# q and k computed as two extra columns of the value projection, with row scales transposed later

## The reference

```python
h = jnp.maximum(_layernorm(x, axis=-1), 0.0)          # over the nodes
q = jnp.einsum('c,bcn->bn', wq, h)
k = jnp.einsum('c,bcn->bn', wk, h)
scores = q[:, None, :] + k[:, :, None]
scores = jnp.where(scores > 0, scores, 0.01 * scores)
att = jax.nn.softmax(scores, axis=-1)
agg = jnp.einsum('bcn,bmn->bcm', h, att)
out = jnp.einsum('oc,bcm->bom', wm, agg) + bm[None, :, None]
x = x + jax.nn.relu(out)
```

## Time and profile before

| | |
|---|---|
| median of 3 runs | 2089.28 us (2089.21 to 2089.91) |
| profiled execution | 2090.47 us, its span 2088.7 |
| TensorE busy | 2051.5 us (98%) |
| VectorE busy | 1674.8 us (80%) |
| ScalarE busy | 1221.5 us (58%) |
| GpSimd busy | 379.6 us (18%) |

### The profile page before, as it was taken

How to read it: one execution, slowest core, us unless ns; L and a number is a source line. 1 busy time by engine, 2 the same in 40 slices (tenths; PEclk the granted TensorE clock), 3 DMA queues, 4 the chain that set the end, 5 groups by cost and what they waited for, 6 DMA issues and landing times.

```text
span 2088.7 us, 33534 instructions
## 1 busy us (share of the span) xinstructions
PE 2051.5 (98%) x10448; PEld 950.3 (45%) x10448; DVE 1674.8 (80%) x3661; ACT 1221.5 (58%) x1871; POOL 379.6 (18%) x273
## 2 busy tenths in 40 slices
PE   5899999999999999999999999999999999999999
PEld 2344444444444444444444444444444444444444
DVE  7978878778887788887788877888877888778853
ACT  5556656556655566565566555665655665556634
POOL 1012211112111122111121111221111211112212
PEclk9999999999999999999999999999999999999999
DMA  5244433344324444333433234442334432343332
GB/s 195 64 155 142 148 99 123 138 160 141 133 84 136 151 141 146 104 118 137 161 141 133 84 136 151 141 146 105 117 137 161 141 131 86 136 152 141 106 101 76
DMA packets 126395, 271.46 MB, mean 130 GB/s; under 512 B 22624, under 2 KB 23136, under 8 KB 122208
## 3 DMA queue, kind: packets, MB, share of 16 engines
q1 hardware_dynamic: 123904, 269.01, 37.1%
q10 hardware_dynamic: 2400, 1.58, 0.3%
HBM read 202.91 MB, written 67.63 MB: 130 GB/s over the span
## 4 chain that ended last, share of the span: by engine, by line
PE 95%; DVE 3%; DMA 1%; POOL 0%; issue 0%; ACT 0%; POOLq 0%; SPq 0%; DVEq 0%
PE mix L385 21%; PE mix L387 21%; PE mix L386 21%; PE mix L362 10%; PE mix L363 10%; PE mix L364 10%; PE small L325 2%; DVE den_out L728 1%; PE small L334 1%; DMA xs<-in_x_dram 0%; DVE p_ring L749 0%; DVE p_lo L756 0%; DVE v_lo L761 0%; POOL wm_nat L893 0%; DMA den_row<-den_rows 0%
## 5 line engine op out<-in xcount | busy, mean ns | idle before, releaser
L385 PE MATMUL mix<-p_hi,v_hi 128*128 128x512 f16 x2048 | 776.3, 379 | 5.9 <-DVE p_lo L756 5.4
L386 PE MATMUL mix<-p_lo,v_hi 128*128 128x512 f16 x2048 | 776.2, 379 | 0.0
L387 PE MATMUL mix<-p_hi,v_lo 128*128 128x512 f16 x2048 | 776.2, 379 | 0.0
L911 POOL TENSOR_TENSOR res<-res,y 128x512 f32<-128x512 f32 x256 | 370.5, 1447 | 1688.2 <-ACT y L512 1688.2
L749 DVE SCALAR_TENSOR_TENSOR p_ring<-ab_row,cols,p_ring 128x512 f32<-128x512 f32 x512 | 377.1, 748 | 129.7 <-ACT p_ring L491 129.7
L491 ACT ACTIVATE p_ring<-ab_row,cols 128x512 f32<-128x512 f32 x512 | 349.5, 691 | 192.4 <-DMA ab_row<-ab_rows 132.3
L503 ACT ACTIVATE v_hi<-mix 128x512 f16<-128x512 f32 x256 | 152.7, 597 | 444.1 <-PE mix L364 443.5
L728 DVE SCALAR_TENSOR_TENSOR den_out<-den_row,cols 128x512 f32<-128x512 f32 x512 | 393.4, 806 | 1.0 <-DMA den_row<-den_rows 1.0
L362 PE MATMUL mix<-wmT_hi,h_hi 128*128 128x512 f16 x1024 | 389.1, 380 | 0.0
L364 PE MATMUL mix<-wmT_hi,h_lo 128*128 128x512 f16 x1024 | 388.8, 380 | 0.0
L363 PE MATMUL mix<-wmT_lo,h_hi 128*128 128x512 f16 x1024 | 388.8, 380 | 0.0
(11 more groups left out here) (71 smaller groups left out, 838.9 us busy)
## 6 DMA issues: line engine op xcount, KB each, us to landing
res<-in_x_dram SPq DMA_DIRECT2D x256, 256.0 KB, 3.2
out_dram<-res SPq DMA_DIRECT2D x256, 256.0 KB, 2.1
xs<-in_x_dram SPq DMA_DIRECT2D x124, 512.0 KB, 6.5
den_row<-den_rows SPq DMA_DIRECT2D x32, 1024.0 KB, 4.6
ab_row<-ab_rows SPq DMA_DIRECT2D x64, 512.0 KB, 5.0
res<-in_x_dram SPq DMA_DIRECT2D x4, 512.0 KB, 5.0
wm_nat<-in_adj_dram ACTq DMA_DIRECT2D x1, 1024.0 KB, 12.2
den_rows<-cols SPq DMA_DIRECT2D x32, 8.0 KB, 1.6
```

Source lines behind the costliest of these rows:

```text
L385: pe.matmul(ps[:, :], v_hi[:, b[1], nt, chans], p_hi[:, hf, nt, :], start=(nt == 0), stop=False)
L386: pe.matmul(ps[:, :], v_hi[:, b[1], nt, chans], p_lo[:, hf, nt, :], start=False, stop=False)
L387: mm = pe.matmul(ps[:, :], v_lo[:, b[1], nt, chans], p_hi[:, hf, nt, :], start=False, stop=(nt == NT - 1))
L911: pool.tensor_tensor(res[:, k, :], res[:, k, :], y[:, k % 2, :], ALU.add).then_inc(s_add, 1)
```

## The change

Two weight columns (wq and wk, scaled and split like wm) are appended to the first half of the transposed weights, so that a projection tile gives q and k in columns 256 and 257 of its first bank. A tile now takes two whole PSUM banks (`pair0` or `pair1`; the four mix banks are the same memory), 258 columns in one and 256 in the other, and so two tiles are in flight where four were. `project_qk` and `select_qk` go; batch 0 alone has its q and k computed ahead of the projection, by 96 products of two columns. ScalarE copies q and k out of the tile ahead of v_hi. `q_head`, `q_tail`, the exponentials and `spread_qmax` move from the projection into the next period (`spread_qmax` to unit 0, ahead of nt 3). The 16 denominator pieces stand behind half 1 of p and no longer between its tiles. `transpose_ab` moves from nt 2 to nt 5 of unit 5. The lower half of v tile 0 moves into half 0 of p. On ScalarE relu 0 to 7 and the parts of h change places. Of the setup, two of the four scalings of wm go from GpSimd to VectorE and the split of wq and wk to GpSimd.

```diff
             def v_tile(b, nt):
-                if nt < MIX and at(b, second):
-                    pe.wait_ge(s_vlo[nt % 2], (nt + MIX) // 2 + 1)
-                elif nt < MIX:
-                    wait(pe, s_y[nt % 2], cnt(b, U // 2, (nt + MIX) // 2 + 1 - U))
+                if nt == 0:
+                    pe.wait_ge(s_hlo, cnt(b, CT, CT))
+                if nt < 2 and at(b, second):
+                    pe.wait_ge(s_vlo[nt], NT // 2)
+                elif nt < 2:
+                    for i in range(2):
+                        wait(pe, s_y[i], cnt(b, U // 2, nt + 3 - U))
                 else:
-                    pe.wait_ge(s_vlo[nt % 2], cnt(b, NT // 2, (nt - MIX) // 2 + 1))
-                ps, nodes = mix[nt % MIX], slice(nt * P, (nt + 1) * P)
+                    pe.wait_ge(s_vlo[nt % 2], cnt(b, NT // 2, nt // 2))
+                ps, nodes = pair[nt % 2], slice(nt * P, (nt + 1) * P)
...
-                    pe.matmul(ps[:, :], hi, wmT_hi[:, ct, :], start=(ct == 0), stop=False)
+                    for half, cols_of in enumerate((OH + QK, OH)):
+                        pe.matmul(ps[:, half, 0:cols_of], hi, wmT_hi[:, ct, half, 0:cols_of],
+                                  start=(ct == 0), stop=False)
...
             def unit(b, k, one):
                 elif one:
-                    pe.wait_ge(s_vlo[k % 2], cnt(nxt(b), NT // 2, (k + MIX) // 2 + 1))
+                    pe.wait_ge(s_vlo[k // 2], cnt(nxt(b), NT // 2, NT // 2))
...
-                    if one and k == MIX + 1 and nt == 2:
+                    if one and k == MIX + 1 and nt == 5:
                         transpose_ab(nxt(b))
+                    if one and (k, nt) == ((1, 2) if at(b, first) else (0, 3)):
+                        spread_qmax(nxt(b))
...
             def v_phase(b):
-                project_qk(b)
                 for nt in range(NT):
-                    if nt == 2:
-                        select_qk(b)
-                    if nt == 4:
-                        spread_qmax(b)
                     v_tile(b, nt)
...
             def v_upper(b, nt):
                 act.wait_ge(s_v, cnt(b, NT, nt + 1))
+                ps = pair[nt % 2]
+                if not at(b, first):
+                    act.activation(qk4[:, nt, :], ps[:, 0, OH:OH + QK], ACT.Copy)
...
             def q_head(b):
+                else:
+                    dve.wait_ge(s_vhi, cnt(b, NT, NT))
+                q_link(b, 1, dve.tensor_scalar(qk[:, 0, :], qk4[:, :, 0], unscale_q[:, 0:1], None, ALU.mult))
...
             def late(b, one, two, three):
                 if two:
-                    q_rows(h)
-                    for nt in range(NT):
+                    for nt in range(1, NT):
                         v_lower(h, nt)
...
-                        if three and nt == 6:
+                        if three and nt == 5:
                             normaliser(nxt(b, 3))
```

More of the change, by code:

```diff
@@ L51, in gnn_layer @@
     RING = 3
[L52 to L54 removed]
+    OH = O // 2
+    QK = 2
     MIX = 4
@@ L313, in transposed_weights, with project_first_qk @@
                             mm.then_inc(s_wt, 1)
[L315 to L335, removed]
+            def project_first_qk():
+                pe.wait_ge(s_wqk, 2)
+                pe.wait_ge(s_hlo, CT)
+                for nt in range(NT):
+                    for ct in range(CT):
+                        nodes = slice(nt * P, (nt + 1) * P)
+                        hi, lo = h_hi[:, 0, ct, nodes], h_lo[:, 0, ct, nodes]
+                        w_hi, w_lo = wmT_hi[:, ct, 0, OH:], wmT_lo[:, ct, 0, OH:]
+                        pe.matmul(qk_ps[:, nt, :], hi, w_hi, start=(ct == 0), stop=False)
+                        pe.matmul(qk_ps[:, nt, :], hi, w_lo, start=False, stop=False)
+                        mm = pe.matmul(qk_ps[:, nt, :], lo, w_hi, start=False, stop=(ct == CT - 1))
                 mm.then_inc(s_qk, 1)
@@ L770, in half_0 @@
                     p_lower(b, nt)
+                    if two and nt == 5:
+                        v_lower(nxt(b), 0)
             def early(b, one, two):
                 h = nxt(b, 2)
+                if one:
+                    q_head(nxt(b))
                 weight(b, NT)
@@ L777, in early @@
                         weight(b, NT + nt + 1)
-                    if one:
+                    p_lower(b, NT + nt)
+                    if one and nt == 0:
+                        q_tail(nxt(b))
+                if one:
+                    for nt in range(NT):
                         denominator(nxt(b), nt)
-                    p_lower(b, NT + nt)
-                if one:
                     row_scales(nxt(b))
@@ L794, in late @@
                 if one:
-                    half_0(nxt(b))
+                    half_0(nxt(b), two)
                 if two:
-                    q_rows(h)
-                    for nt in range(NT):
+                    for nt in range(1, NT):
                         v_lower(h, nt)
-                        if nt == 1:
-                            q_head(h)
-                        if nt == 3:
-                            q_tail(h)
-                        if three and 2 <= nt < 2 + CT:
-                            statistics(nxt(b, 3), nt - 2)
-                        if three and nt == 6:
+                        if three and 1 <= nt < 1 + CT:
+                            statistics(nxt(b, 3), nt - 1)
+                        if three and nt == 5:
                             normaliser(nxt(b, 3))
```

204 lines of the change are left out of this document (95 added, 109 removed).

## The result

The changed kernel takes 2125.93 us (median of 4 runs, 2124.51 to 2127.4) against 2089.24 (4 runs, 2088.99 to 2089.91): ratio 1.0175, 95% interval 1.0158 to 1.0193. It is slower by 36.7 us. The forecast was 2153, with 2105 to 2185 as its range: the sign and the mechanism hold, the loss is a little over half of the one forecast. The profiled execution took 2125.26 us with a span of 2123.5, so 34.8 more than before.

A forecast was written before the change was run, and what follows sets the result against it. TensorE's row was taken as the bound. Per projection -1.44 + 0.35 + 0.05 + 0.3 + 2.7 = +1.96 us, times 30 = +58.8, plus 3.5 start and 1.7 end: +64, median about 2153 us, range 2105 to 2185.

The forecast's parts named there:

- Bound and mechanism: TensorE's own row sets the time; it stands before tile 1 of each projection, waiting for relu 7 on ScalarE.
- Removed, -1.44 a batch: The q/k block (1.08 us) and the select products (0.36) leave TensorE's row: 1.44 us a batch saved.
- Projection in two banks, +0.35: 96 products of 512 columns become pairs of 258 and 256, about 0.2195 us a pair: +0.35 us a batch.
- Rival D: Projection: weight loads do not fit under 256 columns, a product takes say 0.125 us: 2228 us in all; chance 0.04.
- Tile 6 and the normaliser, +0.05: VectorE's normaliser delays tile 6's lower half, which unit 0 needs: 0.05 us counted, bounds 0 to 0.3.
- The maxima's transpose, +0.3: The qmax transpose, 9 products into unit 0, waits for VectorE's maximum: 0.2 to 0.5 us, 0.3 taken.
- Tile 1's wait, +2.7: Tile 1's banks hold units 6 and 7, so it waits for relu 7: 2.7 us in each of 30 projections.
- The transpose bound: Row scales' transpose to relu 7's end, 17.1 us with semaphores, against 15.0 until tile 1 is due: wait 2.1 us.
- Start +3.5, end +1.7: Start: 96 two-column products for first q and k, +3.5 us (-2 to +8); end: batch 31's half 0 late, +1.7.
- Signs in the profile: Tile 1 stand 2 to 3.4 us, period 65 to 66.5, ring's first operation under 6 us before unit 7's end.
- No dip of the clock: A clock dip from TensorE's idle time was left out; an earlier 2.78 us stand at the start had none.
- GpSimd holding VectorE: GpSimd's additions 1 to 3 fall among VectorE's 16 denominator pieces: 3.1 to 3.3 us; or GpSimd loses each time.

The follow-up runs named there:

- experiment 2: Changed kernel with the row scales' transpose back at product 2 of unit 5 and VectorE's copy of the scales ahead of two lower halves of h: 2092.60 us.
- experiment 3: Changed kernel with relu 7 right behind relu 6 on ScalarE and the splits of tiles 0 and 1 later: 2075.11 us.
- experiment 8: Changed kernel with the row scales' transpose at product 2 of unit 5, and GpSimd's additions of units 1 to 3 over 8 columns, not 512: 2075.30 us.
- Experiment 5: Relu-7-early kernel (2075.1 us) with whole 512-column projection products in one bank, q and k columns left out inside the loop: 2063.38 us.
- experiment 6: Relu-7-early kernel (2075.1 us) with the transpose of the maxima of q 9 products later in unit 0: 2073.04 us.

## Why the prediction was right, and where its sizes were off

- *Bound and mechanism.* TensorE's row bounds the kernel, and tile 1 waits for relu 7: shown by the waits, and by experiments 2, 3 and 8. By three different edits they take away three quarters of the stand, all but one short wait, and almost nine tenths.
- *Removed, -1.44 a batch*: holds. With the terms below, the stand left out, 63.83 - 1.44 + 0.55 + 0.08 + 0.12 = 63.14, and a period of experiment 3 is 63.15.
- *Projection in two banks, +0.35*: it is +0.55. A pair starts every 0.2216 us; I had 0.2195 from groups of four narrow products, whose loads were smaller. The Trainium skill (TensorE: Matmul & The Clock Gate, Back-to-back issue gap) gives, as an estimate by its formula, 109.2 and 110.0 ns for the two products, 0.2192 a pair; the trace shows 1% more with a full weight load under each. Rival D is false.
- *Tile 6 and the normaliser, +0.05*: 606.27 to 606.54 is 0.27, so 0.05 there; 0.08 in the mean of 29 batches. Experiment 5 shows how close it was.
- *The maxima's transpose, +0.3*: 0.16 in the batch of experiment 6, 0.12 in the mean.
- *Tile 1's wait, +2.7*: the term that was too large. It is 1.72 in the steady batches (44.9 / 29, and 0.17 of modelled end). The transpose bound alone gave 2.1, and I added 0.6 for a later VectorE. The ring stage ends at U0 + 13.05 (I had 13.7), three pieces are held for 1.0 each as forecast, and the scales are ready at U0 + 27.5 (I had 28.2 to 28.8). With the two lower halves of h VectorE is there just when the transpose is, and the copy comes at U0 + 29.8 (I had 30.7): that is 0.9 of the 1.0. The rest is the way from copy to ring. I took 6.19 from one batch of the earlier trace rows; the mean is 6.0 in both kernels.
- *The sum* is then -1.44 + 0.55 + 0.08 + 0.12 + 1.72 = 1.03 a batch, as measured; 1.96 was forecast. The projection's term was too small by 0.20, those of the maxima's transpose and of tile 1 too large by 0.18 and 0.98, so a part of the error cancels.
- *Start +3.5, end +1.7*: 1.6 and 2.3. The 96 small products took 2.6 us. The first stand before tile 1 is 1.6 longer than the others (3.3 against 1.7), so the rest of the start comes out at about nothing.
- *Signs in the profile.* Three lay just outside what I had named: the stand is 1.7 us (2 to 3.4), the period 64.86 (65 to 66.5), and the ring's first operation comes 6.0 ahead of unit 7's end in the mean, 6.25 in the batch read above (under 6).
- *No dip of the clock*: wrong. In the second projection there are two. TensorE stands 2.16 us (to 69.68), and soon behind it the granted clock is 0.50, the 1.2 GHz level, with pairs 0.43 apart. Then it stands 4.35 us before tile 6, and behind that stand the clock is 0.50 again:

```profile
69.68 0.39 PE L350 MATMUL pair<-wmT_hi,h_hi 128*128 128x258 f16 x2 [2.16 <-DVE v_lo L743]
...
78.33 0.61 PE L350 MATMUL pair<-wmT_hi,h_hi 128*128 128x258 f16 x2 [4.35 <-DVE v_lo L743]
78.74 0.64 PE L353 MATMUL pair<-wmT_lo,h_hi 128*128 128x258 f16 x2
```
```profile
71.00:73.80 2.80, 2.80 (x14) 1.79 (x12) 2.51 (x14) 0.17 (x1) 0.00 (x0) 0.50 1.03 317
78.40:80.80 2.40, 2.40 (x12) 1.69 (x13) 2.39 (x4) 2.05 (x6) 0.00 (x0) 0.50 0.04 10
81.00:84.00 3.00, 3.00 (x29) 2.59 (x28) 3.00 (x5) 2.65 (x6) 0.00 (x0) 0.99 0.00 0
```

  The second costs 1.3 us, once; the first ends in the stand that follows it, which is put down to a split on VectorE, so it probably costs little. The stands of 1.65 in the loop have no such dip; the batch above has 1.00. In the kernel before, a stand of 2.78 us had none, so the length of a stand alone does not tell.
- *GpSimd holding VectorE.* Three of 16 pieces took 1.75 us in place of 0.74, each beside an addition, and small additions undid it. The Trainium skill (SBUF — State Buffer, Who interferes with whom) has two such instructions exclude each other for a whole instruction; the trace agrees (1.75 us beside an addition, 0.74 else). Here each addition got its turn at the next piece (1.46 to 1.62 us, 1.27 undisturbed), without the starving that I had left open.

## What to carry to other kernels

When a change merges buffers, list for each merged buffer its last user's place in the other engines' program order: the wait costs what that place costs, and moving one small instruction (relu 7, with the splits behind it) was worth more than the whole rest of the change. When a result is held by two chains at once, undoing one alone can show almost nothing (4.4 us of 36.7 here); undo both before you acquit one. Read a duration that a wait hangs on over all batches, not from one. A cover of some tenths of a microsecond has to be rechecked when the work that gives it gets shorter.

## What was not expected of the hardware

- 96 products of 2 columns with a full weight load each ran 27 ns apart (25.10 to 27.66), while each load is shown with 104 ns; I had allowed up to 100 ns apiece.

```profile
L317 PEld LDWEIGHTS small<-wmT_hi,h_hi x32: 104/104/105, 25.1 to 27.6; 128*128 128x128 f16 x32
```

- A product of 256 or 258 columns with a full load under it costs 110.8 ns in the mean, half of one of 512 columns (215.8) and 3 ns, so splitting a product in two is not free even where its load is hidden.

- In experiment 2 VectorE took up a finished piece 1.5 to 1.7 us late each time its loop went back to its start, 12 times in all, with 2.8 to 3.3 us between the last instruction of a turn and the first of the next. The other kernels have the same loop, but a longer idle stretch at this place, so nothing of it shows in their times.
